# Four unread TensorE products behind each quad and each window of a graph kernel's sum passes

## The reference

```python
# layer 0, three times
msg_sum = jax.ops.segment_sum(h[src], dst, num_segments=N_NODES)
h = h @ W_self + (msg_sum / deg) @ W_neigh + b
# layer 1: attention of 4 heads
out = jax.ops.segment_sum(xt[row] * alpha[..., None], col, num_segments=n)
# layer 2: four evaluations of f, each over both directions of the edges
k1 = f(x); k2 = f(x + dt * k1 / 3); k3 = f(x + dt * (k2 - k1 / 3)); k4 = f(x + dt * (k1 - k2 + k3))
# layer 3: one of 64 matrices per edge
msg = h_all[src, etypes] * norm
agg = jax.ops.segment_sum(msg, dst, num_segments=x.shape[0])
```

## Time and profile before

| | |
|---|---|
| median of 3 runs | 21753.78 us (21741.98 to 21762.46) |
| the profiled execution | 21875.38 us |
| its span, first to last instruction | 21873.6 us |
| mean granted TensorE clock | 0.614 |
| TensorE busy | 10234.6 us, 47% |
| GpSimd busy | 14143.2 us, 65% |
| VectorE busy | 6368.7 us, 29% |
| ScalarE busy | 2697.4 us, 12% |

### The profile page before, as it was taken

The page is one execution under the profiler, slowest core; times in us unless marked ns, Lnnn a source line. Parts: engine busy times, 40 slices in busy tenths (PEclk is TensorE's granted clock), DMA queues, the critical chain, the costliest instruction groups (busy, mean ns, idle before and its releaser), DMA issues.

```text
span 21873.6 us, 147184 instructions
## 1 busy us (share of the span) xinstructions
PE 10234.6 (47%) x41175; PEld 7163.9 (33%) x41176; DVE 6368.7 (29%) x12754; ACT 2697.4 (12%) x4406; POOL 14143.2 (65%) x14027
## 2 busy tenths in 40 slices
PE   5214444444477634434444444444444344448744
PEld 2113333333222323323333333333333333334333
DVE  8401111111477632222222222222222222226422
ACT  0001101010155421101000011001011001100010
POOL 5876676766755676676666666666666666660365
PEclk8655555555688755555555556555555565658855
DMA  1111211211100011121212112121211212125412
GB/s 31 9 23 46 46 42 46 42 46 47 13 1 1 2 14 46 46 48 46 45 47 43 51 46 46 46 48 46 46 47 46 48 46 46 46 46 211 188 46 45
DMA packets 555319, 1025.63 MB, mean 47 GB/s; under 512 B 276823, under 2 KB 344031, under 8 KB 529110
## 3 DMA queue, kind: packets, MB, share of 16 engines
q0 software_dynamic: 448640, 761.10, 16.4%
q1 hardware_dynamic: 102595, 256.61, 3.1%
q10 hardware_dynamic: 3600, 1.51, 0.0%
HBM read 767.92 MB, written 248.53 MB: 46 GB/s over the span
## 4 chain that ended last, share of the span: by engine, by line
POOL 35%; another core or an unknown queue 20%; issue 20%; PE 12%; DVE 7%; DMA 3%; ACT 2%; DVEq 1%; ACTq 0%; POOLq 0%; SPq 0%
POOL rows L405 28%; POOL list_f L389 5%; PE ps L1011 4%; PE ps L1101 3%; POOL list_r L389 3%; ACT work L462 2%; PE ps L1055 2%; DMA rows<-table,rows_F 1%; DVE onehot L701 1%; DVE rows L715 1%; DVE peak_tile L816 1%; DMA rows<-table,rows_R 1%; PE ps L1052 1%; PE ps L1017 0%
## 5 line engine op out<-in xcount | busy, mean ns | idle before, releaser
L1011 PE MATMUL ps<-rows,onehot 128*128 128x128 f32 (+1 forms) x22880 | 5352.9, 406 | 8395.6 <-DVE rows L715 4747.5
L405 POOL DMA_INDIRECT rows<-table,rows_F x7040 | 6864.8, 975 | 3332.5 <-issue 2028.8
L1011 PEld LDWEIGHTS ps<-rows,onehot 128*128 128x128 f32 x22880 | 4677.5, 299 | 9555.0 <-issue 7950.5
L405 POOL DMA_INDIRECT rows<-table,rows_R x3520 | 3419.8, 972 | 1630.1 <-issue 995.5
L462 ACT COPY work<-ps 128x1188 f32 x1430 | 1641.9, 1148 | 16874.2 <-remote 9132.3
L701 DVE TENSOR_TENSOR onehot<-iota,list_F 128x512 f32<-128x512 f32 x1980 | 1284.5, 690 | 5973.0 <-ACT work L462 3385.1
L1000 PE MATMUL ps<-naught 128*128 128x396 bf16 x4290 | 1592.9, 505 | 1492.3 <-issue 1491.9
L405 POOL DMA_INDIRECT rows<-rel_table,rows_F x880 | 851.6, 968 | 1261.1 <-DMA rel_table<-list_R 856.3
L389 POOL DMA_INDIRECT list_f<-list_F,work x850 | 1064.6, 1252 | 401.6 <-issue 258.7
L413 POOL DMA_INDIRECT rows<-peak_table,rows_F x880 | 831.3, 945 | 761.7 <-PE ps L1055 534.4
L389 POOL DMA_INDIRECT list_r<-list_R,rows_R x850 | 1110.6, 1307 | 259.0 <-issue 259.0
(11 more groups left out here) (198 smaller groups left out, 6211.3 us busy)
## 6 DMA issues: line engine op xcount, KB each, us to landing
rel_table<-list_R SPq DMA_DIRECT2D x196, 1024.0 KB, 3.9
rows<-table,rows_F POOLq DMA_INDIRECT x7040
rows<-table,rows_R POOLq DMA_INDIRECT x3520
table<-H SPq DMA_DIRECT2D x5, 3136.0 KB
rows<-peak_table,rows_F POOLq DMA_INDIRECT x880
rows<-rel_table,rows_F POOLq DMA_INDIRECT x880
list_f<-list_F,work POOLq DMA_INDIRECT x850
list_r<-list_R,rows_R POOLq DMA_INDIRECT x850
```

The costliest lines, as they stand in the source:

```text
L405: pool.indirect_dma_start(out=rows[:, t % UNROLL, 0:FEAT], out_offset=None, in_=from_table, in_offset=bass.IndirectOffsetOnAxis(ap=rows_of ...
L1011: ins = mm(into, onehot[:, s, :], rows[:, s, 0:width], start=False, stop=True, skip_group_check=True)
```

## The change

`keep_clock` issues four products of the identity with itself, repeated four times along the free axis, so 512 fp32 columns each, into bank 7 of PSUM. No instruction reads the result. It is called behind the fourth tile of each window, that is between its two quads, and behind the closing product. Nothing else is changed, and nothing waits for these products or is waited for by them.

```diff
+IDLE_PRODUCTS = 4
...
+            def keep_clock():
+
+                for _ in range(IDLE_PRODUCTS):
+                    mm(ps[:, 7, :].rearrange("p (a b) -> p a b", a=4), ident[:, :], ident[:, :].unsqueeze(1).to_broadcast([P, 4, P]), start=True, stop=True)
+
             def block_sums(name, width=FEAT):
...
                         if j % QUAD == QUAD - 1:
                             ins.then_inc(quad_summed, 1)
+                        if j == QUAD - 1:
+                            keep_clock()
 
                     if m0 + w:
                         pe.wait_ge(window_stored, m0 + w)
                     mm(half[:, 0:width], ident[:, :], sums_flat[key][:, bass.ds(firsts[w % 2], width)],
                        start=False, stop=True, skip_group_check=True).then_inc(window_summed, 1)
+                    keep_clock()
```

## The result

The changed kernel is slower: 21918.65 us (median of 4, 21904.94 to 21924.26) against 21752.96 (median of 4, 21741.98 to 21762.46), a ratio of 1.0079 [1.0063, 1.0094], or 166 us more. The forecast was 21127, faster.

What follows compares the result with a forecast made beforehand. GpSimd's gathers plus 1,912 us of holds were taken as the bound. 21875 - 637 (rarer holds) + 10 (pass ends) = 21248, 627 less; from the median, 21754 - 627 = 21127 us, range 19840 to 23250.

Steps and rivals of the forecast that it cites:

- What bounds the kernel: In the thirteen sum passes, GpSimd's gathers at 1.25 us each plus 1,912 us of its ring waits for TensorE.
- holds: In the passes, about every 34 us, TensorE's completions held back and coming at once, losing GpSimd 4 to 5 us.
- The clock alone buys nothing: In the passes, a quad's sum 0.9 us shorter at full clock only lengthens 9.7 us of slack.
- Price of the bursts: On TensorE at full clock, 3.43 us a burst; a window 9.66 us, just under GpSimd's 10.0.
- Pass ends, 10 us: At pass ends no next gather hides a burst: 0 to 25 us more, taken as 10.
- if the gap matters, holds get rarer; I take a third: At each window's first quad, closing the gap behind the clears saves a third of 1,912 us, 637; chance 0.38.
- Holds are indifferent: Rival: the bursts leave the holds in the passes as they were, 21754 to 21779 us; chance 0.20.
- More holds by instruction count: Rival: TensorE's instruction count sets the holds, 1.76 times as often, 1,457 us more, 23211; chance 0.17.
- at the same price each: In the instruction-count rival, each added hold costs as much as before: 0.76 x 1,912 = 1,457 us more.
- mixed-clock bound: Rival: TensorE at clock 0.88 bounds the passes, 11.9 us a window, +715 us, 22470; chance 0.12.
- half clock: Rival: the clock stays at half, TensorE bounds at 20.2 us a window, 12,580 us more, 34330; chance 0.05.
- 9.7 us of slack: In the passes, time left before GpSimd needs a quad's sum, taken to cover TensorE running about 3 us late.

Runs made afterwards that it cites:

- before_again: The kernel before, unchanged, run again on chip 4: 21745.35 us (one run).
- the first pair: The profiled kernel before and changed kernel of the stated result, chip number unknown: medians 21752.96 and 21918.65 us, ratio 1.0079.
- after_again: The changed kernel, unchanged, run again on chip 4: 21895.64 us, ratio 1.0074 to the kernel before there.
- narrow and half bursts: Passes of one mixed-variant kernel on chip 12, bursts of four 32-column products or two products instead of four; whole kernel 22022.65 us, ratio 1.0131 to the kernel before.
- after_third: The changed kernel, unchanged, run on chip 1: 19837.51 us, ratio 1.0006 to the kernel before there.

## Why the prediction was wrong

**What bounds the kernel: right on this chip, and only there.** GpSimd's gathers at 1.25 us and 1,912 us of ring waits, all of them late completions of TensorE, is what chip 4 shows again (1,785 us in before_again), and chip 12 in its passes without a burst. The reading that the whole excess of a pass is holds is confirmed from the other side: on chips without them the pass is 1,103 us, and the kernel 1,930 us shorter.

**The clock alone buys nothing: right.** On chips 1, 5 and 10 mean clocks of 0.59 to 0.93 bought nothing: the kernels at the higher clock were level by what can be told, or 22 us slower.

**Price of the bursts: right.** 3.43 us a burst was 3.43; a window for TensorE was put at 9.66 and is 9.38, because the two quads take 0.89 each and not 0.99, and the clears 0.51 and not 0.60. The clock rose as forecast, to 0.94 or more in a pass.

**Pass ends, 10 us: too much, harmless.** The last quad of `rk1 R` now starts at 14574.49 behind a gap of 2.18 us, inside a hold; on chip 4 the lengths of the passes account for 160 of 163 us.

**The step that failed: "the first quad follows the clears almost without a gap; if the gap matters, holds get rarer; I take a third".** It gave −637 us. Gaps behind the clears did vanish, as forecast, but the holds came oftener and shorter, and the waits in a pass rose from about 137 to 157 us on chip 4 (147 to 160 in the first pair). The traces settle it over more windows, 963 in nine passes, with the gap before the first quad and the lateness of the copy worked out for each. In before_again 31% of the copies were over 1 us late behind gaps under 0.4 us and 68% behind gaps over 1.1, so the correlation was there. But in after_again 949 of the 963 gaps are under 0.4 us, and 82% of those copies are late. So a hold does not need the gap: without the gaps there are more of them. A correlation of few rows had been given the largest term of the sum.

**The rivals.** "Holds are indifferent" (21754 to 21779) is wrong by 140 us, the forecast by 792. "More holds by instruction count" named the right sign, and count fits the narrow and half bursts better than time does, though not in proportion. Its price was 1,457 us and the cost measured is 163, a ninth. The step that failed there is "at the same price each": holds came at most 24/16 = 1.5 times as often, and "remote" waits 1.3 to 1.4 times (483 to 639 on chip 4, 456 to 636 in the first pair), short of the 1.76 of the count; and each lost less (3.0 us on average to 2.7 on chip 4), so that a gather went from 1.42 to 1.43 us on average. That average, and not the price of one hold, is what stayed nearly the same. The mixed-clock bound and the half clock didn't occur: TensorE at 0.94 to 0.99 stays under GpSimd.

**What stays open.** Why TensorE's completions are held on some chips and not on others; what sets their distance (that it is always a whole number of quads is the kernel's doing: GpSimd waits only before a quad); and why added instructions lengthen them in sum. A late semaphore alone is not the whole of it. The products of a burst wait for nothing, and yet TensorE stood before them in after_again:

```profile
PE ps L993 <- issue: 847.8, 1047, 2.4
```

On chip 1 (after_third) TensorE's list has no such row. So on a chip with holds TensorE also stands with nothing to wait for that the profile shows, here 848 us in 1,047 gaps. What stops it is not shown.

## What to carry to other kernels

A wait that fills 9% of a kernel with no engine's work behind it may belong to the chip: run the unchanged kernel on a second chip before explaining it, let alone tuning for it. Raising TensorE's clock is worth something only where TensorE ends a wait; here it had an estimated 9.7 us of slack, and the filler cost 163 us on a chip with holds (3.6 ns for each of its 45,760 instructions on average, though fewer instructions did not cost in proportion) and 13 to 22 us on one without. And when a ring is freed from one engine, follow the other ties of the new releaser: VectorE hung on the same completions two windows back.

## What the runs showed of the hardware that was not expected

- The same kernel took 21732 us on chips 4 and 12 and 19798, 19825 and 19801 us on chips 5, 1 and 10, 9% apart. The difference is mostly in the passes (1,247 against 1,103 us in `rk1 F`) and in the peak pass's waits for L1064 (512.4 us in after_again, 343.9 in after_third).
- On the first kind the completions of TensorE come late: by 9.9 us in the hold of the earlier trace rows, and by over 1 us in 46% of the windows before and 83% after, against none on chip 1. In a hold they reach GpSimd and ScalarE within 0.05 us of each other, 34.3 us apart before and 22.9 after in the stretches shown.
- On the first kind TensorE also stood 848 us in front of products that wait for nothing; the list of chip 1 has no such wait.
- A product of 512 fp32 columns in the bursts is two records and 0.86 us at full clock. With eight records of 0.43 us a burst TensorE was busy 1107.50 of 1259.60 us in the pass, and its clock there was 0.95 where it had been 0.57. On chip 1 bursts with a bf16 product of one record gave a mean clock of 0.791, those with 32 fp32 columns 0.594, the level of before.
